# Second-mean transfers ordered behind FFN2's pair-1 loads, in a one-core decoder layer

## The reference, cut to what matters

```
x = x + mamba2_block_with_mlp(layernorm(x), ...)      # FFN1 is its gated MLP
x = x + quantised_product(layernorm(x), ctx)          # "ctx stage"
x = x + ffn(layernorm(x), w1, mean_w1, w2, mean_w2, w3, mean_w3)   # FFN2

def _binary_diff_weight(w, base):
    d = w - base
    return base + mean(abs(d)) * sign(d)
W1, W2, W3 = (the above of w1, w2, w3 with their means)
h = silu(x @ W1.T) * (x @ W3.T);  ffn = h @ W2.T      # 1024 -> 3584 -> 1024
```

## Time and profile before

| | us |
|---|---|
| median of 3 runs | 2107.42 (2106.41 to 2109.32) |
| span of the profiled execution, first to last instruction | 2105.5 |
| PE busy in it | 2078.2 |
| DVE busy | 1679.2 |
| ACT busy | 1056.9 |
| POOL busy | 185.3 |
| stretch in which FFN2 starts (PE's step 0 to step 16) | 1293.46 to 1340.49 |

### The profile page before, as it was taken

How to read it: one execution, slowest core, us unless ns; L and a number is a source line. 1 busy time by engine, 2 the same in 40 slices (tenths; PEclk the granted TensorE clock), 3 DMA queues, 4 the chain that set the end, 5 groups by cost and what they waited for, 6 DMA issues and landing times.

```text
span 2105.5 us, 26520 instructions
## 1 busy us (share of the span) xinstructions
PE 2078.2 (99%) x9230; PEld 1669.2 (79%) x9234; DVE 1679.2 (80%) x2528; ACT 1056.9 (50%) x1748; POOL 185.3 (9%) x296
## 2 busy tenths in 40 slices
PE   8999999999999999999999999999999999999999
PEld 4777778788888888888888845788888888888887
DVE  8888686797777888888979899977677776698886
ACT  5333244457777787774444476533333333444442
POOL 0001101101111112110000002010000000100000
PEclk9999999999999999999999999999999999999999
DMA  3151116639889999896430045454444443846101
GB/s 136 40 203 57 51 61 200 145 117 325 292 294 339 325 349 346 294 347 255 148 133 1 1 180 123 163 197 145 174 146 174 159 150 123 323 175 205 55 21 60
DMA packets 136434, 370.07 MB, mean 176 GB/s; under 512 B 16688, under 2 KB 27568, under 8 KB 132656
## 3 DMA queue, kind: packets, MB, share of 16 engines
q1 hardware_dynamic: 110640, 287.12, 39.6%
q0 software_dynamic: 25088, 80.23, 11.3%
q10 hardware_dynamic: 576, 1.05, 0.1%
HBM read 288.12 MB, written 84.41 MB: 177 GB/s over the span
## 4 chain that ended last, share of the span: by engine, by line
PE 87%; DVE 9%; ACT 2%; issue 1%; DMA 1%; ACTq 0%; SPq 0%; DVEq 0%
PE pair L1086 47%; PE pair L1134 24%; PE pair L856 7%; PE pair L1030 2%; DVE conv_out L2172 2%; PE pair L849 1%; PE pair L1096 1%; DVE weights_lo L1737 1%; PE pair L968 1%; PE pair L989 1%; DMA sign_in_ab<-sign_spill 1%; PE pair L1167 1%; PE pair L995 0%; DVE centred L2383 0%; DVE hs L2091 0%
## 5 line engine op out<-in xcount | busy, mean ns | idle before, releaser
L1086 PE MATMUL pair<-comb_hi,ring_hi 128*128 128x512 f32 x1456 | 566.5, 389 | 0.0
L1086 PE MATMUL pair<-comb_lo,ring_hi 128*128 128x512 f32 x1456 | 566.4, 389 | 0.0
L1086 PE MATMUL pair<-comb_hi,ring_lo 128*128 128x512 f32 x1456 | 566.4, 389 | 0.0
L1134 PE MATMUL pair<-inner_ring_a,ring_hi 128*128 128x512 f32 x1080 | 332.5, 389 | 0.0
L1086 PEld LDWEIGHTS pair<-comb_hi,ring_hi 128*128 128x128 f32 x1456 | 273.3, 188 | 57.2 <-issue 0.4
L1086 PEld LDWEIGHTS pair<-comb_hi,ring_lo 128*128 128x128 f32 x1456 | 273.3, 188 | 56.7
L1086 PEld LDWEIGHTS pair<-comb_lo,ring_hi 128*128 128x128 f32 x1456 | 273.3, 188 | 56.6
L1134 PEld LDWEIGHTS pair<-inner_ring_a,ring_hi 128*128 128x128 f32 x1080 | 202.6, 188 | 42.0
L1134 PE MATMUL pair<-inner_ring_a,ring_lo 128*128 128x512 f32 x540 | 210.1, 389 | 0.0
L1360 ACT ACTIVATE ring_hi<-ring_sum 128x512 fp32r<-128x512 f32 x160 | 100.5, 631 | 147.8 <-DVE ring_sum L1820 145.7
L1835 DVE TENSOR_TENSOR ring_lo<-raw_a,ring_hi 128x512 fp32r<-128x512 f32 x146 | 99.6, 688 | 53.4 <-ACT ring_hi L1360 51.6
(11 more groups left out here) (397 smaller groups left out, 3610.0 us busy)
## 6 DMA issues: line engine op xcount, KB each, us to landing
coeff_in<-f_gu SPq DMA_DIRECT2D x56, 512.0 KB, 5.3
coeff_in<-b_gu SPq DMA_DIRECT2D x56, 512.0 KB, 6.9
weights_raw<-w_mamba SPq DMA_DIRECT2D x44, 512.0 KB, 3.5
raw_a<-w_gu SPq DMA_DIRECT2D x28, 512.0 KB, 6.3
raw_a<-w_gu SPq DMA_DIRECT2D x56, 256.0 KB, 6.2
u_spill<-gate_a POOLq DMA_DIRECT2D x56, 256.0 KB, 4.9
coeff_in<-f_dn SPq DMA_DIRECT2D x28, 512.0 KB, 4.7
coeff_in<-b_dn SPq DMA_DIRECT2D x28, 512.0 KB, 6.6
```

The source lines that it names most:

```text
L1086: ins = pe.matmul(out, wt[:, slot, col], a, start=t in (0, 1, 3) and kk == 0 and n == 0, stop=kk == KH - 1 and n == 2, skip_group_check=True)
L1134: ins = pe.matmul(out, wt[:, slot, col], a, start=t in (0, 1, 3) and k == 0 and n == 0, stop=k == SC_PAIRS - 1 and n == 2, skip_group_chec ...
```

## The change

Three edits. SP issues the loads of sign tiles 4 to 7 ahead of the two loads of pair 1. POOL, before its 16 accumulating transfers, waits until both loads of pair 1 have landed. ACT's `move_b22` goes from its turn 12 to turn 16 (and the order in which the high parts are counted follows).

```
-MOVE_AT = 12
+MOVE_AT = 16
...
         spill_x2(0)
         spill_x2(1)
+        for f in range(4, 8):
+            load_sign(f)
         load_second(1, 0)
         load_second(1, 1)
-        for f in range(4, 8):
-            load_sign(f)
...
                 pool.wait_ge(s_x2, 32 * KT)
+                for x in range(2):
+                    pool.wait_ge(s_rc[1][x], 16 * (PAIRS // 2 + 1))
                 for b in range(BATCH):
                     pool.wait_ge(s_m2, b + 1)
                     for o in range(KT):
                         pool.dma_start(x2_spill[o][:, HALF[b]], scr_c(7)[:, HALF[b]], accum_op=ALU.add).then_inc(s_x2a, 16)
```

## The result

The changed kernel takes 2118.23 us in the median of 5 runs (2116.23 to 2118.88), against 2107.42 before: a ratio of 1.0045, interval 1.0034 to 1.0056 (the two medians by themselves give 1.0051). It is slower, as forecast, but by about twice as much: 2112.7 us and a range up to 2115.8 had been given.

A forecast was written before the change was run, and what follows sets the result against it. PE, busy 2078.2 of 2105.5 us, was taken as the bound. Step 20's 4.9 us plus step 21's 0.36 made 5.3 us, DVE's gain no longer counting: 2107.42 + 5.3 = 2112.7 us, range 2107.0 to 2115.8.

The forecast's parts named there:

- the whole path: FFN2: POOL's later accumulates delay ACT's move of b22, then the copy PE's step 20 needs; 5.3 us lost.
- DVE's 1.24 us: DVE's idle time until sign tile 4 lands disappears when sign tiles go out earlier; 1.24 us.
- the move in turn 16: ACT, before the weights of step 21: the 2.18 us move fits the 2.50 us idle gap if T is early enough.
- The rival that the accumulates end in time: Pair 2's loads wait behind POOL's transfers, T is 1344.2 to 1345, so 2106.2 to 2107.4 us; chance 0.17.
- the sharing of the queues: DMA engines alternate between queues with work, a packet at a time, so pair 2's loads slow the accumulates; T is 1350.
- The page's fit of 2.0 us and 436 GB/s for one POOL transfer: Skill's fit, putting the 16 accumulates through in an estimated 11.6 us; the prediction set the trace's 203 GB/s against it.
- T: Landing time of POOL's last accumulate, which ACT's move waits for; taken as 1350, with PE late by T - 1345.1.
- The bound: Upper bound for T: 1350.6, from 30.6 us for the accumulates with as much traffic beside them as before.
- The lower bound: Accumulates with nothing beside them: 24.2 us from first issue, so T is 1344.2.
- That wait of 0.36: PE's step 21 waits 0.36 us more, as ACT's two copies end 3.08 us apart and PE's steps are 2.72 apart.
- the likeliest case: Accumulates late at ACT's move, T from 1349 to 1353, time 2111.6 to 2115.6 us; chance 0.58.
- More is late: Pair 2's first load takes 13 us or more, or T reaches 1353: 8 us lost, 2115.7 us; chance 0.04.

The follow-up runs named there:

- x1: Only the sign tile order changed against the kernel before, without POOL's wait and with the move in turn 12: 2107.40 us, ratio 0.9996.
- x2: Only the move of b22 put in turn 16 against the kernel before, POOL and SP as before: 2107.67 us, ratio 0.9998.
- x7: The changed kernel, but SP holds pair 2's two loads until the accumulates have landed: ratio 1.0017 to the kernel before.
- x10: The changed kernel, with pair 2's loads and POOL's stores of inner values both held until the accumulates have landed: ratio 1.0027 to the kernel before.
- x3: Only POOL's wait added to the kernel before, move in turn 12, sign tiles behind the loads: 2123.46 us, ratio 1.0070.
- x5: The changed kernel, but the 16 accumulates carry another tile, so the move waits only for the second mean: 2108.11 us, ratio 1.0000.
- x6: The changed kernel, with 28 unused matmuls put ahead of step 20's wait on PE: 2116.57 us, ratio 1.0038.
- the second profile: The changed kernel run and profiled once more, with no further edit: 2117.81 us, ratio 1.0041 to the kernel before.

## Why the prediction was wrong

**Right.** The side, and the whole path: sign tiles give DVE's 1.24 us (x1: 1.29); POOL starts on pair 1's second load (forecast at 1320.0, which is 26.5 us behind step 0; measured 1322.45 - 1296.03 = 26.4); the move in turn 16 costs nothing by itself (x2); ACT stands at the move, and from the landing of the last accumulate to the end of the copy it is 1360.28 - 1354.34 = 5.9 us, forecast 6.1; PE stops at step 20 and nowhere later. The rival that the accumulates end in time is out in every run with POOL's wait: even with pair 2's loads held, the last landed 52.9 us behind step 0 (x7), which is 1346.3 in the forecast's times, past its 1345. On the sharing of the queues the Trainium skill (DMA: Bandwidth & Descriptors, Queues, rings and completion order: a packet of each queue in turn) was on the right side, since the accumulates took 26.4 us without pair 2's loads and 31.9 with them. That the trace agrees, as the prediction says, holds for this sharing only: SP's loads moved nothing from 1311.4 to 1315, and from 1315 to 1325 it was 704 packets of SP's queue to 433 of POOL's, not one for one. The page's fit of 2.0 us and 436 GB/s for one POOL transfer (the Trainium skill, the same page, Anatomy of one DMA) was not on the right side: 26.6 us were measured for the sixteen (x10), against the 11.6 estimated from it.

**Wrong: T, the landing of the last accumulate.** The term that was mis-sized is the time that the 16 transfers take beside pair 2's loads: 30.0 us in the sum (1320.0 to 1350), 31.9 and 32.8 measured. "I take T = 1350, near the upper bound" of 1350.6 was 56.5 us behind step 0; it came 58.3 and 59.1 us behind (1354.34 - 1296.03, and 1353.11 - 1293.97). The bound was no bound: it was the 30.6 us of a run in which the loads met only the tail of the 16 transfers, and in the new order, with nearly the same volume on SP's queue while they ran (2.62 MB with the change, 2.50 before, 2.10 in x1), these took 31.3 to 33.6 us in the seven profiles that have POOL's wait and pair 2's loads beside (four in the table; x3 31.3, x5 and x6 32.0). Why they take longer than the 30.6 is not shown. The lower bound, 24.2 us with nothing beside, no run tests: with only sign tiles 8 to 10 beside they take 26.6 (x10), and at the 203 GB/s of the earlier trace rows those tiles' 0.39 MB would take an estimated 1.9 us of that. PE's step 20 started 1.7 us later than forecast (64.35 us behind step 0 against 57.74 + 4.9 = 62.6), and 2.6 in the second profile.

**Missing: the clock.** The sum had PE's idle time and put what follows it at nothing, without a reason. After 7.8 us of idle time step 20 ran at half clock for its first matmuls: from there to the end 752.57 us against 751.12 before (1351.20 to 2102.32), 1.45 us, and 2.25 in the second profile (753.37), where the forecast had 0.36 for the second copy. That wait of 0.36 did not come: the second copy was done at 1363.4, and the slowed step 20 ran until 1364.8.

So 5.3 us forecast, plus 1.7 for T, plus 1.1 for the clock, make the 8.1 of the first profile's stretch; in the second it is 5.26 + 2.56 + 1.89, the 9.7 there. T alone would not have left the range: in the forecast's times it came at 1351.8 and 1352.6, within the 1349 to 1353 of the likeliest case, which by the forecast's sum is 2114.5 to 2115.3. With the clock it is 2115.5 by the first profile, just inside the range that ended at 2115.8, and 2117.1 by the second, outside it. The medians lie 10.8 us apart, and 8.8 in the second measurement (2117.81 against 2108.97); the interval of the first ratio, 7.2 to 11.8 us, holds these and both stretches, and no row explains the differences between them. "More is late" was not what came: DVE never waited for pair 2's loads, and T stayed below 1353.

## What to carry to other kernels

A wait added to ease a crowd moves the crowd: here it won nothing beyond what reordering the small transfers won alone, and it made late the one thing that an engine in the critical order waited for. Before giving a transfer a later start, look up who waits for its end, add up what will meet it in its new place, and don't take the duration of a transfer that met a crowd at its tail as the upper bound for one that meets it earlier: here it was passed by 0.7 to 3.0 us in all seven profiles. And ask for every PE idle time in a forecast what it costs in clock besides its length: here one of 2.3 us had such a price as well as one of 7.8.

## What the runs showed of the hardware that was not expected

Accumulating transfers and loads slow each other down by much: the 4.2 MB of the accumulates took 26.6 us with only three sign tiles beside (x10) and 31.3 to 33.6 us with two 1 MB loads as well, and these took 12.1 and 13.3 us to land with the change, where one such load alone takes 4.9. PE's granted clock went from full to half within an idle time of 7.8 us and came back some 3.4 us into the next step, in the second profile (8.63 us) some 5 us into it. After an idle time of only 2.34 us (x7) it fell to half as well, when PE was already running again. With 6.5 us of matmuls in the gap and 1.04 us of idle time left (x6), it stayed full.
